# Second biases added while mixing by products over 128 rows, scales for eight tiles at once, output gates carried in the record

## The chip, the core and the metric

The kernel is one program on one core of a Trainium2 chip. A core has TensorE (PE; its weight loads are PEld), VectorE (DVE), ScalarE (ACT), GpSimd (POOL) and SyncE (SP, which here only issues DMAs). The metric is the device time of one execution in microseconds (us), lower is better.

## The reference

Eight sequences of 512 tokens with 256 features pass through one block: `x + s * g`. `s` is a recurrent attention layer with 16 heads of 16, `g` a mixture of eight experts, two per token.

```python
xn = _layernorm(x)
# attention: per token and head
q = silu(xn @ Wq); k = l2_norm(silu(xn @ Wk)); v = xn @ Wv
f = sigmoid(xn @ Wf1 @ Wf2);  a = -k * sigmoid(xn @ Wgamma) * f
def step(S):                    # 512 steps, one after the other
    S = S * f[..., None]
    S = S + k[..., None] * ((a @ S) + v)[..., None, :]
    return S, q @ S             # o
o = o * sigmoid(xn @ Wog1 @ Wog2)                 # the output gate
s = (o - mean(o)) * rsqrt(var(o) + 1e-5) * norm_w @ Wo
# experts: the two best of softmax(xn @ Wg + bg), weights cw
y = sum_e cw[:, e] * (gelu(xn @ W1[e] + b1[e]) @ W2[e] + b2[e])
g = silu((y - mean(y)) / sqrt(var(y) + 1e-5) * gamma + beta)
return x + s * g
```

## The kernel before

A **tile** is 128 tokens: 16 consecutive time steps of the eight sequences; there are 32. The recurrence has partition = (sequence, head), so its 512 steps are serial. DVE takes two steps at once: a **pair** g, 256 of them, eight to a **chunk** c of 16 time steps (`two_steps` L1167 to pair 55, `two_shared_steps` L1207 after it, where POOL computes the products of the state with decay, a and q, L310 to L327). Chunk c of the recurrence has the same tokens as tile c.

**Head.** Per tile, PE projects, ACT and DVE form a record of five rows of 16 (a, f, k, q, v), which SP writes to DRAM (`spill`, L362) and reads back in the recurrence's layout (`load_chunk`, L370). The output gate goes to DRAM by itself (`og_d`, L364). A record slot is used again four tiles later, so ACT and DVE wait for the write of tile n-4. From tile 4 on, this work stands between the operations of pairs 0 to 28. Then DVE routes the tokens (`route`, L1037), POOL scatters them to the experts' rows and the experts start.

**Experts.** 39 tiles of 256 rows: PE multiplies by W1 (L891), ACT applies gelu, PE multiplies by W2 (L903) and adds b2 as a product with one row of ones (L905); ACT scales the result by the token's weight (L723); POOL writes it to its token's row (`land`, L522). POOL runs its own list in order, so *when* it lands a result is a table in the code: landing number `landed` stands after the products of the first pair with (g-56)*PAIR_STEP >= landed//2*LAND_STEP, one per pair. A table of when, not a wait: POOL does it there, no earlier.

**Mixing and output**, woven into pairs 224 to 255. For each j of 16 (two tiles): PE adds the two experts' rows (`add_experts`, L914), ACT takes mean and squares (`moments`, L757), POOL the scale (`spreads`, L533), ACT normalizes (`normed`), PE transposes, ACT applies silu with gamma and beta (`silu_g`), PE transposes back, ACT copies g out (`turned_back`). For each tile n: SP fetches o and the gate, DVE multiplies them (`gate_o`, L1104) and takes statistics (`out_stats`), every four tiles their spread (`out_spread`), POOL the scales (`out_scales`), ACT normalizes, PE transposes and multiplies by Wo (`out_rows`, L949, products L959), DVE multiplies with g (`gated`, L1118), POOL adds x (`sum_up`), SP stores. In pair 224+n DVE does gate_o(n) and out_stats(n), and gated(n-5): **the recurrence waits in pair 229 for the output row of tile 0**, in pair 230 for tile 1, and so on. After pair 255 the last tile's output follows alone.

Of the kernel before, what the change touches and what calls it, by code (L numbers as in the profile page):

```python
# [19 lines left out]
REC = 5 * HD  # L20
A_, F_, K_, Q_, V_ = (HD * n for n in range(5))
# [23 lines left out]
YR = 3  # L45
SR = 4
RB = 3
SHARED = 7
LAND0, LAND_STEP = 390.0, 15.9
PAIR_STEP = 3.7  # L50


def build(nc, x, wq, wk, wv, wgamma, wf1, wf2, wog1, wog2, norm_w, wo,
          wg, bg, w1, b1, w2, b2, gamma, beta, out):
    ctx = ExitStack()
    with ctx:
# [6 lines left out]
        def sem(name):  # L63
# [6 lines left out]
        og_d = nc.dram_tensor("og_d", [NT, P, D], F32, kind="Internal").ap()  # L70
# [19 lines left out]
        b2_sb = sb("b2_sb", [1, E, D])  # L90
# [21 lines left out]
        ogs = work[:, o1 + 6 * D:o1 + 10 * D].rearrange("p (u n) -> p u n", u=RS)  # L112
        ksq = work[:, o1 + 10 * D:o1 + 11 * D]
# [54 lines left out]
        oTs = xTs  # L168
        sel = gw[:, 0, :, :].rearrange("p t e -> p (t e)")
        b2_flat = b2_sb[:, :, :].rearrange("a e n -> a (e n)")  # L170
        f_on = work[:, 0:FR * D].rearrange("p (u d) -> p u d", u=FR)
        fog, fx, f_sg = (work[:, (FR + n * SL) * D:(FR + (n + 1) * SL) * D].rearrange("p (u d) -> p u d", u=SL)
                         for n in range(3))
# [23 lines left out]
        s_og = sem("s_og")  # L197
# [11 lines left out]
        s_ogd = [sem(f"s_ogd{n}") for n in range(RS)]  # L209
# [10 lines left out]
        s_b1t = sem("s_b1t")  # L220
        s_b1 = sem("s_b1")
# [30 lines left out]
        s_o = sem("s_o")  # L252
        s_od = [sem(f"s_od{n}") for n in range(OB)]
        s_fl = [sem(f"s_fl{n}") for n in range(SL)]
        s_mul = sem("s_mul")
# [25 lines left out]
        N_W, N_C = 10, 9  # L281
# [16 lines left out]
        def shared(g):  # L298
            return g // NP >= SHARED

# [31 lines left out]
        def _(sp):  # L332
# [21 lines left out]
            sp.dma_start(b2_sb[:, :, :], b2.rearrange("(a e) n -> a e n", a=1)).then_inc(s_c, 16)  # L354
# [4 lines left out]
            sp.wait_ge(s_pool0, 4)  # L359
# [13 lines left out]
            def store_chunk(c):  # L373
                sp.dma_start(o_w[c], obh[:, c % OB, :, :]).then_inc(s_od[c % OB], 16)

            def next_chunk(c):
                sp.wait_ge(s_o, (c + 1) * RING)
                sp.wait_ge(s_recd[(c + RB) % RS], 16 * ((c + RB) // RS + 1))
                load_chunk(c + RB, c % RB)

            for n in range(NT):
# [6 lines left out]
                done, at = divmod(n - HEAD + 1, NP)  # L388
# [10 lines left out]
            for u in range(RS):  # L399
                sp.wait_ge(s_ogd[u], 16 * (NT // RS))  # L400

            def fetch(n):
# [19 lines left out]
            for s in range((NCH - WOVEN) * NP):  # L422
# [6 lines left out]
                if s % NP == 0:  # L429
                    c = WOVEN + s // NP - 1  # L430
                    sp.wait_ge(s_o, (c + 1) * RING)
# [3 lines left out]
            sp.wait_ge(s_o, NCH * RING)  # L435
# [10 lines left out]
        def _(pool):  # L446
# [6 lines left out]
                      channel_multiplier=ZR, allow_small_or_imprecise_dtypes=True).then_inc(s_pool0, 1)  # L453
            pool.memset(ident[:, :], 0.0).then_inc(s_id, 1)
# [78 lines left out]
            def spreads(j):  # L533
                lo, hi = 2 * j, 2 * j + 2
                pool.wait_ge(s_sq, hi)
                pool.tensor_scalar(ysq[:, lo:hi], ysq[:, lo:hi], 1.0 / D, EPS, ALU.mult, ALU.add).then_inc(s_yp, 1)
                pool.wait_ge(s_yp, 2 * j + 1)
                pool.tensor_tensor(yrs[:, lo:hi], ysq[:, lo:hi], neghalf[:, lo:hi], ALU.pow).then_inc(s_yp, 1)
                pool.wait_ge(s_yp, 2 * j + 2)
                pool.wait_ge(s_ynm, j + 1)  # L540
# [29 lines left out]
            def prepare_part(c, part):  # L570

# [7 lines left out]
                qa = rows[:, :, Q_:Q_ + 4 * HD].rearrange("p n (s w) -> p n s w", s=2)[:, :, :, 0:HD]  # L579
                fk = rows[:, :, F_:F_ + 2 * HD].rearrange("p n (s w) -> p n s w", s=2)  # L580
# [11 lines left out]
            landed = 0  # L592
            for g in range(SHARED * NP, T // 2):
# [726 lines left out]
```

## Time and profile before

| | us |
|---|---|
| median of 3 runs | 1239.25 (1235.51 to 1239.74) |
| the profiled execution: its time | 1238.9 |
| its span in the trace | 1237.2 |
| DVE busy in it | 1119.4 (90%), 3502 instructions |
| PE busy | 938.7 (76%) |
| POOL busy | 918.9 (74%) |
| ACT busy | 395.7 (32%) |
| DMA | 202.60 MB, 163 GB/s over the span |

The span is what the trace covers; 1.7 us of the execution lie outside it. The trace lists each instruction with its start and duration; neighbours on one engine overlap a little, so the distance between two starts says more than a duration. "[0.65 <-POOL prod_a L310]" means that the engine stood idle for 0.65 us before the instruction and what ended that. The chain of waits follows the work that ended last backwards.

### The profile page before, as it was taken

To read this page: it belongs to the slowest core of one execution; us is meant where nothing else is said; L and a number is where in the kernel's file an instruction comes from. 1 tells how busy PE (TensorE), PEld (TensorE's weight loads), DVE (VectorE), ACT (ScalarE), POOL (GpSimd) and SP (SyncE) were. 2 spreads that over 40 slices of the span, in tenths; PEclk is the share of its full clock that TensorE was granted. 3 is DMA by queue.
4 is the path that set the end of the run, shared out by engine and by line. 5 is a ranking of instruction groups with operands and counts; after the bars stand their busy time and mean duration, and the time that the engine had idled before them with its cause. 6 is when DMAs were issued, how large, how long until landed. Compare 5 with 4: busy or idle time off the path is not lost.

```text
span 1237.2 us, 17465 instructions
## 1 busy us (share of the span) xinstructions
PE 938.7 (76%) x3773; PEld 683.6 (55%) x3774; DVE 1119.4 (90%) x3502; ACT 395.7 (32%) x1047; POOL 918.9 (74%) x902
## 2 busy tenths in 40 slices
PE   5798898100029999999999999999999934667663
PEld 2343343000018888778888777888878723445441
DVE  3799999999999999999999999999999995988882
ACT  3444444200003333332232223333322203554552
POOL 3766666367844888888888888888888884877762
PEclk9888988655559999999999999999999976777787
DMA  5666656553335666655666556666666427355322
GB/s 165 194 209 177 213 180 188 140 191 107 111 94 150 191 196 195 195 170 183 191 195 193 174 177 195 196 187 181 183 192 191 120 67 210 93 157 149 99 81 69
DMA packets 247251, 202.60 MB, mean 164 GB/s; under 512 B 141425, under 2 KB 225233, under 8 KB 247185
## 3 DMA queue, kind: packets, MB, share of 16 engines
q1 hardware_dynamic: 170146, 82.81, 25.5%
q10 hardware_dynamic: 70224, 100.49, 24.8%
q0 software_dynamic: 6816, 18.69, 4.6%
q14 instruction: 55, 0.45, 0.1%
q8 instruction: 10, 0.16, 0.1%
HBM read 139.42 MB, written 62.54 MB: 163 GB/s over the span
## 4 chain that ended last, share of the span: by engine, by line
POOL 36%; DVE 27%; issue 16%; PE 7%; DMA 6%; SPq 3%; ACT 3%; POOLq 0%; DVEq 0%; ACTq 0%
POOL prod_q L327 13%; POOL prod_a L310 12%; POOL y_d L530 5%; DMA rec_d<-work 4%; DVE obh L1164 3%; PE psA L959 3%; DVE ubuf L1180 3%; DVE prod_a L1175 2%; PE psF L921 2%; SPq L335 2%; DVE prod_q L316 1%; DVE prod_a L1198 1%; DVE state L1204 1%; DVE outer L1190 1%; POOL cross L583 1%
## 5 line engine op out<-in xcount | busy, mean ns | idle before, releaser
L310 POOL TENSOR_TENSOR prod_a<-state,rbh 128x512 f32<-128x512 f32 x200 | 254.7, 1274 | 96.2 <-DVE state L1237 74.0
L903 PE MATMUL psF<-wts,work 128*128 128x256 f32 x1248 | 289.1, 385 | 3.2 <-ACT work L712 2.0
L891 PE MATMUL psA<-xgT,wts 128*128 128x256 f32 x1248 | 282.3, 384 | 0.9 <-ACT xgT L706 0.8
L891 PEld LDWEIGHTS psA<-xgT,wts 128*128 128x128 f32 x1248 | 235.4, 191 | 45.1 <-issue 13.8
L903 PEld LDWEIGHTS psF<-wts,work 128*128 128x128 f32 x1248 | 230.8, 190 | 50.0 <-issue 16.5
L327 POOL TENSOR_TENSOR prod_q<-state,rbh 128x512 f32<-128x512 f32 x175 | 223.2, 1276 | 0.0
L1164 DVE TENSOR_REDUCE obh<-prod_q 128x16 f32<-128x272 f32 x512 | 217.6, 426 | 0.0
L712 ACT ACTIVATE work<-psA,b_sb 128x256 f32<-128x256 f32 x312 | 130.8, 470 | 162.3 <-PE psA L891 159.5
L1224 DVE TENSOR_REDUCE ubuf<-prod_a 128x16 f32<-128x272 f32 x200 | 86.0, 430 | 37.5 <-POOL prod_a L310 37.1
L723 ACT ACTIVATE work<-psF,work 128x256 f32<-128x256 f32 x78 | 36.9, 473 | 256.9 <-PE psF L905 256.9
L879 PE MATMUL psT<-ident,work 128*128 128x128 f32 x156 | 24.2, 279 | 119.2 <-DMA work<-xs_d 119.1
L484 POOL TENSOR_TENSOR rinv<-ssm,neghalf 128x16 f32<-128x16 f32 x32 | 100.3, 3134 | 2.7
L502 POOL DMA_INDIRECT xs_d<-x_acc,idx x64 | 79.2, 1237 | 19.5 <-issue 18.9
L1237 DVE TENSOR_TENSOR state<-psB,outer 128x256 f32<-128x256 f32 x200 | 84.2, 421 | 5.8
L1216 DVE TENSOR_TENSOR prod_a<-state,psT 128x256 f32<-128x256 f32 x200 | 83.8, 419 | 5.8
L879 PEld LDWEIGHTS psT<-ident,work 128*128 128x128 f32 x156 | 19.2, 143 | 125.6 <-issue 117.9
L530 POOL DMA_INDIRECT y_d<-work,ids x78 | 78.9, 1011 | 12.3 <-issue 10.0
L1219 DVE TENSOR_REDUCE psB<-prod_a 128x16 f32<-128x272 f32 x200 | 86.5, 432 | 0.0
L1222 DVE TENSOR_TENSOR psB<-rbh,psB 128x256 f32<-128x256 f32 x200 | 83.6, 418 | 0.0
L1230 DVE TENSOR_TENSOR psB<-prod_a,psB 128x256 f32<-128x256 f32 x200 | 83.4, 417 | 0.0
L1232 DVE TENSOR_TENSOR outer<-rbh,psB 128x256 f32<-128x256 f32 x200 | 82.4, 412 | 0.0
L845 PE MATMUL psA<-w_kq,xTs 128*128 128x512 f32 x128 | 78.4, 743 | 0.0
(171 smaller groups left out, 1543.3 us busy)
## 6 DMA issues: line engine op xcount, KB each, us to landing
wts<-in_L_ffn_W_dram ACTq DMA_DIRECT2D x78, 1024.0 KB
rec_d<-work SPq DMA_DIRECT2D x32, 640.0 KB
rbh<-rec_d SPq DMA_DIRECT2D x32, 640.0 KB
xs_d<-zero SPq DMA_DIRECT2D x26, 387.0 KB, 9.0
work<-xs_d ACTq DMA_DIRECT2D x39, 258.0 KB
wts<-y_d ACTq DMA_DIRECT2D x16, 512.0 KB, 5.5
x_acc<-in_L_attn_x_dram SPq DMA_DIRECT2D x32, 128.0 KB
og_d<-work SPq DMA_DIRECT2D x32, 128.0 KB, 7.9
```

The source lines that it names most:

```text
L310: eng.tensor_tensor(prod_a[:, n, 1:3, :, 0:HD], state[:, g % SR, :, :].unsqueeze(1).broadcast_to(wide), rows.unsqueeze(2).broadcast_to(wid ...
L327: eng.tensor_tensor(prod_q[:, g % SR, :, :, 0:HD], state[:, g % SR, :, :].unsqueeze(1).broadcast_to(wide), rbh[:, u, 2 * n - 1:2 * n + 1, ...
L484: pool.tensor_tensor(rinv[:, u, :], ssm[:, u, :], neghalf[:, 0:H], ALU.pow).then_inc(s_ng, 1)
L530: pool.indirect_dma_start(y_d, bass.IndirectOffsetOnAxis(ids[:, v, q:q + 1], 0), ysb[v][:, q, :], None).then_inc(s_yd[v], 16)
L712: act.activation(hT[:, m, :], psA[m // 2 % 2][:, m % 2 * MT:(m % 2 + 1) * MT], ACT.Gelu, bias=b1_sb[:, bass.ds(e * FC + m, 1)]).then_inc(s ...
L891: mm = pe.matmul(psA[m // 2 % 2][:, m % 2 * MT:(m % 2 + 1) * MT], w1_sb[v][:, c, m * P:(m + 1) * P], xgT[:, c, :], start=(c == 0), stop=(c ...
L903: pe.matmul(psF[q][:, 0:D], hT[:, m, q * P:(q + 1) * P], w2_sb[v][:, m, :], start=(m == 0), stop=False)
L1164: dve.tensor_reduce(obh[:, c % OB, row % RING, :], prod_q[:, g % SR, side, :, :], AX.X, ALU.add).then_inc(s_o, 1)
L1216: dve.tensor_tensor(prod_a[:, n, 0, :, 0:HD], old, over_v(home_a[:, n, :]), ALU.mult).then_inc(s_chain, 1)
L1219: dve.tensor_reduce(u1, prod_a[:, n, 0, :, :], AX.X, ALU.add).then_inc(s_chain, 1)
L1224: dve.tensor_reduce(raw, prod_a[:, n, 2, :, :], AX.X, ALU.add).then_inc(s_chain, 1)
L1237: dve.tensor_tensor(new, home_o, outer[:, 1, :, :], ALU.add).then_inc(s_chain, 1)
```

## The change

1. **Second biases.** The one-row product per half expert tile (L905) and the register load for it go. Instead DVE forms the table of weights token x expert (two products and a sum in `route`), ACT spreads it, PE transposes it (during the scatter), and `add_experts` adds one more product per tile with all 128 rows: weights of four tiles' tokens against b2, which stands four times in `b2_sb` with zeros between. b2 is loaded by sixteen DMAs of eight rows in place of one, on SP's list, ahead of the first `spill`.
2. **Scales for eight tiles.** `spreads` takes eight tiles (four calls in place of sixteen), at pairs set by the table `SPREADS`. `moments` also copies the sums to `x_acc`, so `normed` reads them later. PE and ACT do the mixing in four quarters; **output rows begin in the last quarter**.
3. **Gates in the record.** The record has six rows. One product per chunk (`gate_outputs`) multiplies the chunk's outputs before they are stored: on DVE in chunks 1 to 7, on POOL after the products of each chunk's fourth pair from then on. `og_d`, its writes and reads, and `gate_o` go. A record slot is loaded again only after that product. POOL's `prepare_part` and `out_scales` move one pair later.
4. LAND_STEP 15.9 to 15.0 and PAIR_STEP 3.7 to 3.82: the last landing stands at pair 207 in place of 221.

```diff
-REC = 5 * HD
+REC = 6 * HD
+GQ = 8
+SPREADS = (612.0, 624.0, 640.0, 662.0)
+GATED = 3
-LAND0, LAND_STEP = 390.0, 15.9
-PAIR_STEP = 3.7
+LAND0, LAND_STEP = 390.0, 15.0
+PAIR_STEP = 3.82
+        def gate_outputs(eng, c):
+            eng.tensor_tensor(obh[:, c % OB, :, :], obh[:, c % OB, :, :], rbh[:, c % RB, :, O_:O_ + HD], ALU.mult)\
+                .then_inc(s_og, 1)
-            sp.dma_start(b2_sb[:, :, :], b2.rearrange("(a e) n -> a e n", a=1)).then_inc(s_c, 16)
+            sp.wait_ge(s_pool0, 5)
+            for n in range(P // E):
+                sp.dma_start(b2_sb[n * E:(n + 1) * E, n % 4, :], b2).then_inc(s_c, 16)
             def spill(n):
-                sp.wait_ge(s_og, n + 1)
-                sp.dma_start(og_d[n], ogs[:, u4, :]).then_inc(s_ogd[u4], 16)
             def store_chunk(c):
+                sp.wait_ge(s_og, c + 1)
             def fetch(n):
-                sp.dma_start(fog[:, n % SL, :], og_d[n]).then_inc(s_fl[n % SL], 16)
@@ POOL, after the products of pair g
-                if 3 <= g % NP < 6 and g // NP + 1 < NCH:
-                    prepare_part(g // NP + 1, g % NP - 3)
+                if g % NP == GATED and g // NP > SHARED:
+                    pool.wait_ge(s_o, g // NP * RING)
+                    gate_outputs(pool, g // NP - 1)
+                if 4 <= g % NP < 7 and g // NP + 1 < NCH:
+                    prepare_part(g // NP + 1, g % NP - 4)
                 s = g - WOVEN * NP
+                if spread < NT // GQ and ((g - SHARED * NP) * PAIR_STEP >= SPREADS[spread] or s >= 2):
+                    spreads(spread)
+                    spread += 1
-                        if s == hi - 1 and s < NT - 1:
+                        if s == hi:
                             out_scales(q)
-                    if s % 2 == 0:
-                        spreads(s // 2)
@@ ACT
-            moments(0)
-            for j in range(NT // 2):
-                normed(j)
-                ...
+            half = GQ // 2
+            for j in range(2 * half):
+                moments(j)
+            for q in range(NT // GQ):
+                act.wait_ge(s_yr, q + 1)
+                for j in range(q * half, (q + 1) * half):
+                    normed(j)
+                for j in range((q + 2) * half, min((q + 3) * half, NT // 2)):
+                    moments(j)
+                for j in range(q * half, (q + 1) * half):
+                    silu_g(j)
+                    ...
@@ PE
-                    pe.matmul(psF[q][:, 0:D], ones[0:1, :], b2_flat[:, bass.ds(e * D, D)], start=False, stop=True)\
-                        .then_inc(s_y, 1)
+                    mm.then_inc(s_y, 1)
             def add_experts(j):
+                    pe.matmul(total, cwT[:, n // 4, :], b2_sb[:, n % 4, :], start=True, stop=False)
+            for q in range(NT // GQ):
+                for j in range((q + 2) * half, min((q + 3) * half, NT // 2)):
+                    add_experts(j)
+                for j in range(q * half, (q + 1) * half):
+                    turn_y(j)
+                    turn_back(j)
+                    if q == NT // GQ - 1:
+                        for n in range(2 * (j % half), 2 * (j % half) + 2):
+                            out_rows(n)
+            for n in range(GQ, NT):
                 out_rows(n)
@@ DVE
-                if out_tile is not None and out_tile < NT - 1:
-                    gate_o(out_tile)
+                    if n == GATED and 0 < c <= SHARED:
+                        dve.wait_ge(s_o, c * RING)
+                        gate_outputs(dve, c - 1)
```

**What moves on PE.** Before, after the experts' last tile, one j in the middle of the mixing (L921 adds the experts, L933 and L943 are the transposes there and back, L953 and L959 the output row of one tile):

```order
L921 MATMUL psF<-wts,ident 128x256 x4
L933 MATMUL psT<-ident,wts 128x128 x4
L943 MATMUL psB<-ident,gT 128x128 x4
L953 MATMUL psT<-ident,work 128x128 x2
L959 MATMUL psA<-wo_sb,xTs 128x256 x2
L953 MATMUL psT<-ident,work 128x128 x2
L959 MATMUL psA<-wo_sb,xTs 128x256 x2
```

Now, the end of the third and the start of the fourth quarter on PE (L958 and L968 the transposes, L978 and L984 the output row):

```order
L958 MATMUL psT<-ident,wts 128x128 x4
L968 MATMUL psB<-ident,gT 128x128 x4
L958 MATMUL psT<-ident,wts 128x128 x4
L968 MATMUL psB<-ident,gT 128x128 x4
L978 MATMUL psT<-ident,work 128x128 x2
L984 MATMUL psA<-wo_sb,xTs 128x256 x2
L978 MATMUL psT<-ident,work 128x128 x2
L984 MATMUL psA<-wo_sb,xTs 128x256 x2
```

Two output rows followed every j, from the second on; now twelve j pass with none, four with two each, and 24 rows stand alone at the end. All additions of the experts stand ahead of the third quarter.

**What moves on POOL.** Pairs 226 and 227 before (L310 and L327 the products of a pair, L536 to L541 one `spreads` of two tiles, L583 the first `prepare_part`, L561 `out_scales`):

```order
L310 TENSOR_TENSOR prod_a<-state,rbh 128x32x16
L327 TENSOR_TENSOR prod_q<-state,rbh 128x32x16
L536 TENSOR_SCALAR ysq<-ysq 128x2
L538 TENSOR_TENSOR yrs<-ysq,neghalf 128x2
L541 TENSOR_TENSOR ysh<-ynm,yrs 128x2
L310 TENSOR_TENSOR prod_a<-state,rbh 128x32x16
L327 TENSOR_TENSOR prod_q<-state,rbh 128x32x16
L583 TENSOR_TENSOR cross<-rbh 128x8x2x16
L561 TENSOR_TENSOR rstd<-var,neghalf 128x4
L563 TENSOR_TENSOR shift<-nmean,rstd 128x4
```

An ordinary chunk on POOL now, from the fourth pair's products on (L318 and L335 are the products, L306 `gate_outputs`, L587 to L593 the parts of `prepare_part`):

```order
L318 TENSOR_TENSOR prod_a<-state,rbh 128x32x16
L335 TENSOR_TENSOR prod_q<-state,rbh 128x32x16
L306 TENSOR_TENSOR obh<-obh,rbh 128x256
L318 TENSOR_TENSOR prod_a<-state,rbh 128x32x16
L335 TENSOR_TENSOR prod_q<-state,rbh 128x32x16
L587 TENSOR_TENSOR cross<-rbh 128x8x2x16
L318 TENSOR_TENSOR prod_a<-state,rbh 128x32x16
L335 TENSOR_TENSOR prod_q<-state,rbh 128x32x16
L590 TENSOR_TENSOR rbh<-rbh 128x8x2x16
```

Three pairs of a chunk carried an extra product, now four in a row do. Of the four `spreads`, the last stands after the products of pair 226 and needs the squares of all 32 tiles.

## Rows read from the trace of the kernel before

**Rows 1.** The page, 40 slices of the span: DVE's busy tenths and TensorE's granted clock.
```profile
DVE  3799999999999999999999999999999995988882
PEclk9888988655559999999999999999999976777787
```

**Rows 2.** Timeline of DVE (start, duration): pairs alone, and first instructions of chunks 8 and 28.
```profile
721.54 0.42 DVE L1216 TENSOR_TENSOR prod_a<-state,psT 128x256 f32<-128x256 f32 x1
725.10 0.42 DVE L1216 TENSOR_TENSOR prod_a<-state,psT 128x256 f32<-128x256 f32 x1
...
414.46 0.38 DVE L1148 COPY prod_a<-rbh 128x256 f32<-128x256 f32 x1
...
1020.93 0.38 DVE L1148 COPY prod_a<-rbh 128x256 f32<-128x256 f32 x1
```

**Rows 3.** Timeline of one pair with a landing and a `prepare_part` on POOL.
```profile
701.60 1.01 POOL L530 DMA_INDIRECT y_d<-work,ids  x1 [0.17 <-issue]
...
702.64 0.73 POOL L583 TENSOR_TENSOR cross<-rbh 128x256 f32<-128x256 f32 x1
...
704.63 0.43 DVE L1224 TENSOR_REDUCE ubuf<-prod_a 128x16 f32<-128x272 f32 x1 [0.65 <-POOL prod_a L310]
```

**Rows 4.** Timeline of SP and DVE in the head.
```profile
28.62 0.45 SPq L354 DMA_DIRECT2D b_sb<-in_L_ffn_b_dram  x1
...
48.22 0.23 DVE L1130 TENSOR_TENSOR cross<-rbh 128x128 f32<-128x128 f32 x1
```

**Rows 5.** Chain of waits in the head (start, us, what).
```profile
31.45 6.50 DMA rec_d<-work
...
59.39 8.00 DMA rec_d<-work
```

**Rows 6.** Timeline of DVE in `route`.
```profile
246.57 0.42 DVE L1082 COPY tot<-psT 128x256 f32<-128x256 f32 x1 [1.16 <-PE psT L872]
```

**Rows 7.** Timeline of PE: an expert tile's start, a bias product and what follows, the mixing's start.
```profile
384.08 7.17 PE L891 MATMUL psA<-xgT,wts 128*128 128x256 f32 x32
...
719.04 0.69 PE L905 MATMUL psF<-b_sb,ones 1*128 x2
719.66 3.72 PE L903 MATMUL psF<-wts,work 128*128 128x256 f32 x16
...
1024.71 5.79 PE L921 MATMUL psF<-wts,ident 128*128 128x256 f32 x16 [23.94 <-DMA wts<-y_d]
```

**Rows 8.** Timeline of POOL: the last landing.
```profile
1012.60 1.01 POOL L530 DMA_INDIRECT y_d<-work,ids  x1 [0.17 <-issue]
```

**Rows 9.** Chain of waits in the mixing, one j.
```profile
1105.50 2.76 PE psF L921 x8
...
1110.41 0.92 ACT gT L784 x2
...
1111.37 1.11 PE psB L943 x4
...
1113.39 2.07 PE psA L959 x4
...
1116.36 1.76 PE psA L959 x4
```

**Rows 10.** Timeline of DVE among the output tiles, and pair 255's state.
```profile
1034.91 0.41 DVE L1237 TENSOR_TENSOR state<-psB,outer 128x256 f32<-128x256 f32 x1
...
1038.89 0.40 DVE L1237 TENSOR_TENSOR state<-psB,outer 128x256 f32<-128x256 f32 x1
...
1060.95 0.41 DVE L1123 TENSOR_TENSOR work<-psA,x_acc 128x256 f32<-128x256 f32 x1
...
1209.40 0.42 DVE L1237 TENSOR_TENSOR state<-psB,outer 128x256 f32<-128x256 f32 x1
```

**Rows 11.** Groups of instructions by line: busy us and mean ns of one.
```profile
L310 POOL TENSOR_TENSOR prod_a<-state,rbh 128x512 f32<-128x512 f32 x200 | 254.7, 1274 | 96.2 <-DVE state L1237 74.0 <-DVE psT L1141 21.0
L776 ACT ACTIVATE wts<-psF,ysh,yrs 128x256 f32<-128x256 f32 x32 | 16.4, 570 | 1.8 <-POOL ysh L541 1.7
```

More of the change, by code:

```diff
@@ L19 @@
 NTB = T // P
-REC = 5 * HD
-A_, F_, K_, Q_, V_ = (HD * n for n in range(5))
+REC = 6 * HD
+A_, F_, O_, K_, Q_, V_ = (HD * n for n in range(6))
 MT = 256
@@ L208, in build @@
         s_recd = [sem(f"s_recd{n}") for n in range(RS)]
-        s_ogd = [sem(f"s_ogd{n}") for n in range(RS)]
         s_gt = sem("s_gt")
@@ L591, in _ @@
             number(0)
-            landed = 0
+            landed = spread = 0
             for g in range(SHARED * NP, T // 2):
@@ L684, in _ @@
             act.wait_ge(s_b1, 1)
+            act.wait_ge(s_cw, 1)
+            act.activation(cw4.rearrange("p n (r k) -> p n r k", r=4),
+                           gw[:, 1, :, :].rearrange("p (n t) e -> p n (t e)", t=4).unsqueeze(2).broadcast_to([P, NT // 4, 4, 4 * E]),
+                           ACT.Copy).then_inc(s_cw4, 1)
+            act.wait_ge(s_cwT, 1)
+            for n in range(2):
+                act.activation(cwT[:, 4 * n:4 * n + 4, :].rearrange("p n t -> p (n t)"), psA[n][:, :], ACT.Copy, scale=0.25)\
+                    .then_inc(s_cws, 1)
             act.wait_ge(s_slot, 2)
@@ L688, in _ @@
                 act.wait_ge(s_recd[u], 16 * (NT // RS))
-            for u in range(RS):
-                act.wait_ge(s_ogd[u], 16 * (NT // RS))
             def expert_of(t):
@@ L760, in moments @@
                 for n in range(lo, hi):
-                    if j > 0:
-                        act.wait_ge(s_sq, n - 1)
-                    act.activation(junk[:, n % 2, :], summed(n), ACT.Copy, accum_out=ysum[:, n:n + 1]).then_inc(s_sum, 1)
+                    act.activation(x_acc[:, n, 0:D], summed(n), ACT.Copy, accum_out=ysum[:, n:n + 1]).then_inc(s_sum, 1)
+                if j % 2 == 1 and j // 2 + YR < NT // GM:
+                    load_y(j // 2 + YR)
                 act.wait_ge(s_sum, hi)
@@ L805, in _ @@
                 load_y(g)
-            moments(0)
-            for j in range(NT // 2):
-                normed(j)
-                if j % 2 == 1 and j // 2 + YR < NT // GM:
-                    act.wait_ge(s_yab, j + 1)
-                    load_y(j // 2 + YR)
-                if j + 1 < NT // 2:
-                    moments(j + 1)
-                silu_g(j)
-                if j > 0:
-                    for n in (2 * j - 2, 2 * j - 1):
+            half = GQ // 2
[9 more added lines that the diff above has]
+                    silu_g(j)
+                    if q < NT // GQ - 1:
+                        if j > q * half:
+                            turned_back(j - 1)
+                    else:
+                        n = 2 * (j % half)
                         out_normed(n)
+                        out_normed(n + 1)
                         out_turned(n)
-                turned_back(j)
-            for n in range(NT - 2, NT):
+                        turned_back(j)
+                        out_turned(n + 1)
+                if q < NT // GQ - 1:
+                    turned_back((q + 1) * half - 1)
+            for n in range(GQ, NT):
                 out_normed(n)
@@ L872, in _ @@
             pe.matmul(psT[1][:, 0:NT * E], ones[:, :], sel, start=True, stop=True).then_inc(s_cnt, 1)
+            pe.wait_ge(s_cw4, 1)
+            for n in range(NT // 4):
+                mm = pe.transpose(psA[n // 4][:, n % 4 * P:(n % 4 + 1) * P], cw4[:, n, :], ident[:, :])
+            mm.then_inc(s_cwT, 1)
             pe.wait_ge(s_slot, 2)
+            pe.wait_ge(s_cws, 2)
             def turn_rows(t, v, nth):
@@ L1284, in _ @@
             sum_row(T // 2, 0)
+            dve.wait_ge(s_o, NCH * RING)
+            gate_outputs(dve, NCH - 1)
             for n in range((NCH - WOVEN) * NP - LAG, NT - 1):
                 gated(n)
-            gate_o(NT - 1)
             out_stats(NT - 1)
```

105 lines of the change are left out of this document (48 added, 57 removed).

## The prediction

> **What bounds the kernel now.** First the page's slices [rows 1]: DVE is at nine tenths or more in 33 of 40, so the time is mostly the recurrence, one chain of 256 pairs on DVE. The slices that matter are the last seven, where DVE falls to eight tenths and TensorE's clock from 0.9 or more to 0.6 to 0.7. Then the timeline of DVE for the price of a pair. Alone it takes 725.10 - 721.54 = 3.56 us; from chunk 8 to chunk 28 it takes (1020.93 - 414.46) / 160 = 3.79 [rows 2], because a chunk adds its own small operations and because POOL is late when a landing and a `prepare_part` meet: 1.0 and 0.7 us beside the products, and DVE stands 0.65 us [rows 3]. In the last stage 26 pairs, from the first output row that DVE needs (`gated(0)`, pair 229, 1060.95) to pair 255's state (1209.40), take 148.5 us, 5.7 each, though a pair with its statistics and one more operation takes 1038.89 - 1034.91 = 3.98 [rows 10]. The chain of waits says why: there it runs through PE and ACT, the additions, the moments, silu, two transposes and two output rows one behind the other [rows 9]. After pair 255 come 1237.2 - 1209.8 = 27.4 us for the last tile.
>
> So the end is set by five terms: when pair 56 starts; when the last landing is made; from there to `gated(0)`; 26 pairs; 27.4 us.
>
> **Head: 9 us later.** b2 now takes sixteen DMAs on SP where it took one of 0.45 us [rows 4]; with the distance between such issues fifteen more are about 15 x 0.49 = 7.3 us, ahead of the first `spill`. The gate's own DMA goes (0.5). So record 0 leaves at 31.45 + 6.8 = 38.2 instead of 31.45, and takes 6.5 us [rows 5], perhaps 0.8 more for a sixth row. Its read-back starts at 45.5 instead of 38. Before, DVE began chunk 0 at 48.22 [rows 4], so the read-back took at most 10.2 us; if it takes 6, chunk 0 starts at 51.5. Behind it SP is serial for three tiles: record 3 left at 59.39 and landed 8.00 later [rows 5], and DVE's tile 7 (pair 3) waits for it. With 6.8 from the start, no gate DMA (0.5 a tile less) and a larger record it lands 6 to 7 us later. DVE has no idle time afterwards that would give this back [rows 1]. I take 6.5; bounds 1 (the read-back is quick and the queue drains faster without the gates) and 10. Six gate products on DVE ahead of pair 56, in chunks 1 to 6: 128x256 operations of 0.41 us [rows 10], a little less where they overlap their neighbours, 6 x 0.38 = 2.3. `route` gains four operations, three of 0.42 like the one in [rows 6] and smaller ones, some 1.6 us, but DVE stood 1.16 us for PE there: 0.4. Hidden elsewhere: the larger memset on POOL, ACT's joint sigmoid (one operation less), the transposes of the weight table, which lie beside the scatter. In all pair 56 starts 6.5 + 2.3 + 0.4 = 9 us later, bounds 3 and 13.
>
> The Trainium skill ("DMA: Bandwidth & Descriptors", Rules for kernel authors) says to coalesce small transfers, since below 64 KB mostly overhead is paid; here one transfer of 64 KB in total is split into sixteen of 8 KB. It speaks against this edit, and by its figure of some 2 us fixed for each, if they were serial, an estimate would be 30 us. The row bears out only an issue every half microsecond, and SP waits for none of them, so I keep 7.3.
>
> **Last landing: 37 us earlier.** A bias product costs PE 719.66 - 719.04 = 0.62 us [rows 7], two per tile, 1.25. The 38 tiles from 384.08 to the experts' end at 1024.71 - 23.94 = 1000.8 took 16.2 each; they will take 15.0. But POOL lands by its table: the last landing ended at 1012.60 + 1.01 = 1013.6 [rows 8], in pair 221, 13 us behind PE. It now stands in pair 207: 14 pairs or 53.1 us earlier. Against that 9 us from the head, and slower pairs: the gate product makes four of eight pairs heavy instead of three, 0.73 us [rows 3] on a POOL that has 3.56 - 2 x 1.27 = 1.0 us beside its two products [rows 11] and often a landing of 1.0 in it; half of it reaches DVE, 0.36 us a chunk, 0.045 a pair (bounds 0 and 0.09), 151 x 0.045 = 6.8. Last landing 1013.6 - 53.1 + 9 + 6.8 = 976.3. From there to the first addition took 1024.71 - 1013.6 = 11.1 [rows 7, 8]: 987.4, 37 us earlier than before.
>
> **From the first addition to `gated(0)`: 106 us instead of 36.** This is what the change pays. Before, output row 0 followed the second j. Now eight `moments` come first. PE needs 12 products per j in place of 8, 1.5 times the 2.76 of [rows 9], less when the clock is up, 2.7 to 4.1; with two cold ones 26.5 for eight. Eight `normed`: 0.57 each [rows 11], started 0.47 apart, 3.9. Four more `moments` 10.4. Four times silu and both transposes: per j 0.92 for silu, 0.7 to 1.1 for the way back [rows 9], as much for the way there, 0.6 for the copy of g, which PE waits for (an estimate, as for a `normed`): 3.4, and 13.6 plus a table load: 14. Second quarter 3.9 + 9.8 + 12.8, third 3.9 + 12.8, then 3.9 + 1.0 for the first silu and 3.6 for norm, transpose and product of row 0. Sum 106.6; bounds 97 (3.0 per silu cycle, warm) and 118 (3.9 and cold additions). `gated(0)` at 987.4 + 106.6 = 1094, where it was at 1061. DVE gets to pair 229 some 20 us before and stands. The last `spreads` holds POOL at pair 226 until the 32nd square, 30 us before that: it costs nothing, because pair 229 waits longer.
>
> TensorE's clock was 0.9 and more of full speed through the experts and 0.6 to 0.7 in this stage [rows 1]. The Trainium skill ("TensorE: Matmul & The Clock Gate", What's actually happening) has it that the throttled state is the default and activity lifts it. The trace agrees; with the long run of silu cycles, where PE idles more than before, its rule would lean to the upper bound of 118.
>
> **26 pairs: 115 us instead of 148.5.** `gate_o` is gone, with it its waits for the gate's transfer; per pair remain statistics and `gated`: 3.98 [rows 10], 103.5. Six or seven spreads of seven small operations, each under the 0.23 of [rows 4] and overlapping by half, 0.7 together: 4.5. Three chunks with 30.32 - 28.5 = 1.8 us each beyond the pairs [rows 2]: 5.4 (30.32 is eight pairs at 3.79, 28.5 eight at 3.56). For `out_scales` beside a gate or `prepare_part` on POOL 1.5. Sum 115. PE keeps up: without the additions two rows and a j cost about 8.5, 4.2 a row, and later 1116.36 - 1113.39 = 3.0 a row [rows 9]. Bounds 110 and 130. Pair 255's state at 1094 + 115 = 1209, before 1209.4.
>
> **The rest: 27.4 us.** `gate_outputs(31)` comes before the store and `gate_o(31)` goes after the fetch, both 0.4. Bounds 26 and 29.
>
> Sum: 987.4 + 106.6 + 115 + 27.4 = 1236.4 as span, 1238 with the 1.7 us outside it. The profiled execution had 1238.9 and the runs a median of 1239.25. Forecast 1238: 37 us won by the earlier landing are spent on rows that start 70 us later after it, and what the faster pairs give (33) goes on the same account.
>
> **Rivals.** *Faster: the mixing runs warm and the head hides its DMAs.* Then the head costs 3, the stage to `gated(0)` 97 and the pairs 111: 6 + 9.6 + 4 = 19.6 less, 1218; with half of this 1228. For it: single pieces of PE at twice the speed of others in [rows 9] (1.76 beside 2.07, 1.11), record 3's 8 us. Against: the clock digits.
>
> *Slower: the scales come too late for every group of four.* `out_scales` moved from pair hi-1 to hi, and `gated(lo)` stands at the end of hi+1. From the state before pair hi: products 2.5, a part 0.7, scales 1.4, normalize 0.65, transpose, copy and product 3.0, hand-overs 0.5: 8.8, against 0.7 + 2 x 3.98 = 8.7 for DVE. If POOL is one product late or PE cold, DVE waits 1.5 to 3 us in six or seven groups: +15, 1253. It decides from about 0.3 us of lateness on. For it: POOL's lateness in [rows 3]; against: the rows' product was as often 1.76.
>
> *Slower: the experts don't get faster*, because the rows' loads set the tile's length. Then the landings wait on POOL, the last is at about 1010, `gated(0)` 25 to 30 later: 1265. For it nothing in these rows: a bias product has the next product 0.62 behind it [rows 7], so PE goes straight on, and its clock stays up through the stage [rows 1].
>
> **How the numbers follow.** About 0.5% or 6 us is what a measurement of this kernel can tell from no change, so same is 1233 to 1245.5. Forecast 0.47, its own range 1228 to 1248 (0.35 same, 0.06 faster, 0.06 slower). Warm and hidden 0.28 (0.25 faster, 0.03 same). Late scales 0.14 (0.12 slower, 0.02 same). Experts no faster 0.06, slower. The other 0.05: 0.02, 0.01, 0.02. Faster 0.33, same 0.41, slower 0.26. The range reaches into both sides, 1221 to 1254.
>
> **What would show it.** Chunk 0 starting at 51 to 52 on DVE; pair 56 at 394; expert tiles 15.0 apart; last landing at 976; DVE idle 20 us or more in pair 229, ended by PE's output row near 1094; then 4.4 us a pair and no wait for a transfer of o. Wrong if `gated(0)` is at 1080 or earlier, if DVE waits in each group of four for PE, or if landings wait for ACT.

## The result, and the profile after

| | before | after |
|---|---|---|
| median us | 1239.5 (1235.5 to 1241.7, 4 runs) | 1257.6 (1255.6 to 1260.0, 4 runs) |
| profiled execution: time, span | 1238.9, 1237.2 | 1258.4, 1256.7 |
| ratio of the runs | | 1.015, 95% interval 1.013 to 1.017 |

The change makes the kernel 18 us slower. The forecast was 1238, the range 1221 to 1254: both missed, the range by 4 us.

The page after, the lines that answer [rows 1]:

```profile
DVE  3769999999999999999999999999999996479993
PEclk9778889655559999999999999999999687566656
```

Before, DVE was at five tenths in slice 34 and at eight in slices 36 to 39. Now the hole runs over slices 34 to 36 (six, four and seven tenths), and DVE is at nine tenths again from slice 37 on. (The prediction counted 33 slices at nine tenths in the kernel before; there are 32.) PE's clock falls one slice earlier, in slice 32, and is at five or six tenths from slice 35 on, where it was at seven or eight. The timelines (start, duration) give the five terms. First the head, SP and DVE, against [rows 4, 5]:

```profile
28.76 5.84 SPq L364 DMA_DIRECT2D b_sb<-in_L_ffn_b_dram  x16
36.55 0.63 SPq L375 DMA_DIRECT2D rec_d<-work  x1
44.08 0.38 SPq L378 DMA_DIRECT2D rbh<-rec_d  x1
46.34 0.60 SPq L375 DMA_DIRECT2D rec_d<-work  x1
54.98 0.38 SPq L378 DMA_DIRECT2D rbh<-rec_d  x1
...
49.28 0.29 DVE L1158 TENSOR_TENSOR cross<-rbh 128x128 f32<-128x128 f32 x1 [0.83 <-DMA rbh<-rec_d]
...
65.73 0.69 DVE L1041 TENSOR_TENSOR work<-psA,work 128x512 f32<-128x512 f32 x1 [3.25 <-DMA rec_d<-work]
...
78.29 0.69 DVE L1041 TENSOR_TENSOR work<-psA,work 128x512 f32<-128x512 f32 x1 [6.59 <-DMA rec_d<-work]
...
397.28 0.42 DVE L1242 TENSOR_TENSOR prod_a<-state,psT 128x256 f32<-128x256 f32 x1
```

Chunk 0 starts only 1 us later, but SP's list is serial for three tiles: write a record, wait for it to land, read it back. DVE then waits 3.25 and 6.59 us for records to land, pair 3 starts at 78.89 instead of 68.37, and pair 56 (last row) at 397.28 instead of 385.06: 12.2 us. Then the experts, the last landing and the first addition, against [rows 7, 8], and `gated(0)` and the last state, against [rows 10]:

```profile
391.11 7.07 PE L919 MATMUL psA<-xgT,wts 128*128 128x256 f32 x32
405.36 7.07 PE L919 MATMUL psA<-xgT,wts 128*128 128x256 f32 x32
...
980.88 1.01 POOL L535 DMA_INDIRECT y_d<-work,ids  x1 [0.17 <-issue]
...
988.91 1.22 PE L947 MATMUL psF<-b_sb,w_kq 128*128 128x256 f32 x2 [22.06 <-DMA wts<-y_d]
...
1104.85 0.42 DVE L1151 TENSOR_TENSOR work<-psA,x_acc 128x256 f32<-128x256 f32 x1 [23.09 <-PE psA L984]
...
1230.43 0.42 DVE L1263 TENSOR_TENSOR state<-psB,outer 128x256 f32<-128x256 f32 x1
```

| term | forecast | measured |
|---|---|---|
| head: pair 56 later by | 9 | 12.2 |
| a pair from chunk 8 to 28 | 3.84 | 3.84 |
| end of the last landing | 976.3 | 981.9 |
| from there to the first addition | 11.1 | 7.0 |
| first addition to `gated(0)` | 106.6 | 115.9 |
| `gated(0)` to pair 255's state | 115 | 125.6 |
| from there to the end of the span | 27.4 | 26.3 |

The last two rows count from the start of pair 255's state. The forecast's 27.4 was read from its end; measured in that way the last row is 25.9.

Where the additional 10.6 us of the 26 pairs are is seen at the end of a group of four tiles. DVE and POOL there:

```profile
1132.51 0.41 DVE L1151 TENSOR_TENSOR work<-psA,x_acc 128x256 f32<-128x256 f32 x1
1132.84 1.11 DVE L1009 TENSOR_TENSOR lt<-stats 128x4 f32<-128x4 f32 x1
1133.87 0.15 DVE L1010 TENSOR_TENSOR lt<-stats 128x4 f32<-128x4 f32 x1
1133.94 1.23 DVE L1011 TENSOR_TENSOR lt<-stats 128x4 f32<-128x4 f32 x1
1135.10 0.15 DVE L1013 SCALAR_TENSOR_TENSOR lt<-lt 128x4 f32<-128x4 f32 x1
1135.17 0.70 DVE L1016 TENSOR_SCALAR nmean<-lt 128x4 f32<-128x4 f32 x1
...
1136.05 0.41 DVE L1242 TENSOR_TENSOR prod_a<-state,psT 128x256 f32<-128x256 f32 x1
...
1132.67 1.26 POOL L318 TENSOR_TENSOR prod_a<-state,rbh 128x512 f32<-128x512 f32 x1
1133.88 1.27 POOL L335 TENSOR_TENSOR prod_q<-state,rbh 128x512 f32<-128x512 f32 x1
1135.12 0.73 POOL L587 TENSOR_TENSOR cross<-rbh 128x256 f32<-128x256 f32 x1
...
1139.85 1.27 POOL L318 TENSOR_TENSOR prod_a<-state,rbh 128x512 f32<-128x512 f32 x1 [1.59 <-DVE state L1263]
...
1140.01 0.41 DVE L1242 TENSOR_TENSOR prod_a<-state,psT 128x256 f32<-128x256 f32 x1
```

This spread of seven operations on four numbers per partition takes 1136.05 - 1132.84 = 3.2 us. Three of the seven are long, and each ends where an operation of POOL ends: 1133.95 beside 1133.93, 1135.17 beside 1135.15, 1135.87 beside 1135.85. The seven spreads between `gated(0)` and pair 255's state take 1.8, 3.2, 2.7, 3.2, 2.7, 2.7 and 2.7 us, 19.1 in all: where POOL has fewer operations beside a spread, or shorter ones, fewer of the seven are long. In the kernel before the same seven took 0.15 each, 0.7 in all:

```profile
1071.83 0.14 DVE L981 TENSOR_TENSOR lt<-stats 128x4 f32<-128x4 f32 x1
1071.90 0.15 DVE L982 TENSOR_TENSOR lt<-stats 128x4 f32<-128x4 f32 x1
...
1072.43 0.17 DVE L1116 TENSOR_SCALAR var<-lt 128x4 f32<-128x4 f32 x1
...
1072.68 1.01 POOL L561 TENSOR_TENSOR rstd<-var,neghalf 128x4 f32<-128x4 f32 x1 [3.61 <-DVE var L1116]
```

The last row tells why: before, POOL stood during the spread, because `out_scales` was next in its list and waits for it. The change moves `out_scales` a pair later, so POOL runs the next pair's products beside the spread.

The Trainium skill ("SBUF — State Buffer", Who interferes with whom) says that a DVE instruction with two inputs in SBUF contends with a GpSimd instruction that reads SBUF, that a `tensor_scalar` in a two-port mode can contend with GpSimd too, and that the one that comes second waits for the whole of the other. The trace agrees, at 1.11, 1.23 and 0.70 us: POOL's operation had begun each time, while L1010, which began just ahead of POOL's L335, took 0.15. The recurrence's operation that reads one of its inputs from PSUM keeps its 0.41 beside POOL's product (the last two rows).

### The profile page after: what moved, and what is told of

It reads as the page before. It is cut to its first block, busy times and chain, and to the rows that moved or that the text cites. A ratio compares the mean times of both kernels' runs of the same rounds, so it can differ in the third digit from the quotient of the medians.

```text
span 1256.7 us, 16942 instructions
## 1 busy us (share of the span) xinstructions
PE 911.4 (73%) x3689; PEld 688.8 (55%) x3689; DVE 1122.4 (89%) x3482; ACT 402.7 (32%) x1018; POOL 926.2 (74%) x891
## 4 chain that ended last, share of the span: by engine, by line
POOL 35%; DVE 33%; issue 17%; PE 4%; DMA 4%; ACT 3%; SPq 3%; POOLq 0%; DVEq 0%; ACTq 0%
POOL prod_q L335 13%; POOL prod_a L318 10%; POOL y_d L535 5%; DVE obh L1192 4%; DVE ubuf L1208 3%; DVE prod_a L1203 3%; DMA rec_d<-work 2%; SPq L343 2%; DVE prod_a L1226 1%; DVE state L1232 1%; DVE prod_q L324 1%; DVE work L1041 1%; DVE outer L1218 1%; PE psB L968 1%; DVE psB L1245 1%
## 5 line engine op out<-in xcount | busy, mean ns | idle before, releaser
L318 POOL TENSOR_TENSOR prod_a<-state,rbh 128x512 f32<-128x512 f32 x200 | 254.4, 1272 | 115.4 <-DVE state L1263 89.6
L930 PE MATMUL psF<-wts,work 128*128 128x256 f32 x1248 | 279.1, 383 | 0.0
L919 PEld LDWEIGHTS psA<-xgT,wts 128*128 128x128 f32 x1248 | 237.4, 192 | 44.8 <-ACT work L725 12.3
L930 PEld LDWEIGHTS psF<-wts,work 128*128 128x128 f32 x1248 | 236.9, 192 | 30.8
L335 POOL TENSOR_TENSOR prod_q<-state,rbh 128x512 f32<-128x512 f32 x175 | 222.0, 1269 | 0.0
L868 PE MATMUL psA<-w_kq,xTs 128*128 128x512 f32 x128 | 81.8, 773 | 0.0
```

What stands on the lines that cost most here:

```text
L318: eng.tensor_tensor(prod_a[:, n, 1:3, :, 0:HD], state[:, g % SR, :, :].unsqueeze(1).broadcast_to(wide), rows.unsqueeze(2).broadcast_to(wid ...
L335: eng.tensor_tensor(prod_q[:, g % SR, :, :, 0:HD], state[:, g % SR, :, :].unsqueeze(1).broadcast_to(wide), rbh[:, u, 2 * n - 1:2 * n + 1, ...
L919: mm = pe.matmul(psA[m // 2 % 2][:, m % 2 * MT:(m % 2 + 1) * MT], w1_sb[v][:, c, m * P:(m + 1) * P], xgT[:, c, :], start=(c == 0), stop=(c ...
L930: mm = pe.matmul(psF[q][:, 0:D], hT[:, m, q * P:(q + 1) * P], w2_sb[v][:, m, :], start=(m == 0), stop=(m == FC - 1))
```

## The experiments

Every edit is against the kernel after unless said. Times are medians; kernels that ran together share their runs of before (1240.0, 1240.6, 1240.0, 1242.0).

**1 and 2: b2's sixteen transfers.** Once taken out of the way, once put into the kernel before.

```diff
 late_b2
-            for n in range(P // E):            # ahead of spill(0)
-                sp.dma_start(b2_sb[n * E:(n + 1) * E, n % 4, :], b2)
+                if 8 <= n < 12:                # behind spill(n)
+                    for k in range(4 * (n - 8), 4 * (n - 8) + 4):
+                        sp.dma_start(b2_sb[k * E:(k + 1) * E, k % 4, :], b2)
 before_b2x16, in the kernel before
+            for n in range(P // E):            # ahead of spill(0)
+                sp.dma_start(wts[n * E:(n + 1) * E, n % 4 * D:(n % 4 + 1) * D], b2)
```

> The kernel after, with the sixteen b2 transfers moved on SP's list from ahead of the first record to behind records 8 to 11, four each. Theory (SP's queue): the issues hold record 0 back by 5.1 us and everything on the recurrence behind it; chunk 0 starts near 48.3, pair 3 near 73, pair 56 at 391 to 392 instead of 397.3, and the time falls by 5 to 6 us to 1252. Rival (the larger record): the sixth row makes each record's write slower and SP serial; then pair 56 moves by 0 to 2 us and the time is 1256 to 1258.

> The kernel before, with sixteen more transfers of b2 (into a part of the experts' weight buffer that is unused then) on SP's list ahead of the first record; nothing else. SP's queue alone: 16 x 0.37 = 5.9 us, less 0 to 1 of slack; pair 56 at 390 to 391 instead of 385.1 and the time 1244 to 1246. If DMAs are hidden: 1239 to 1241. If they were the whole of the head's 12.2 us: 1250.

Measured: 1252.2 (1.010 of before, 1.008 to 1.011), 5.4 less than after; and 1244.8 (1.0043, 1.0030 to 1.0056), 4.8 more than before. Pair 3 starts at:

| | b2 once or late | sixteen ahead |
|---|---|---|
| record of five rows | 68.37 | 75.11 |
| record of six rows | 72.22 | 78.89 |

Sixteen transfers cost 6.7 us with either record, the kernel with the sixth row 3.8 us with either list. Of the 6.7 us, 5.3 (kernel after) and 5.9 (kernel before) are record 0's later start on SP; the later records then took longer to land (46.36 to 54.02 instead of 40.34 to 47.51, for one), and why is open. Of the sixth row the timelines of SP show the price itself: records 0, 1 and 2 take 7.5, 8.1 and 8.0 us from issue to read-back in late_b2, and 6.5, 7.2 and 7.0 in the kernel before. Pair 56 follows: 391.81 in the kernel before with the transfers, 390.69 in the one after without. What is left to 385.06 is 5.6: 3.8 of the record, and 1.8 of the gate products and `route`. The effects on the time (4.8 and 5.4) are smaller than those on pair 56 (6.7 and 6.6). In before_b2x16 `gated(0)` is 6.2 us later and pair 255's state 4.2, so the last stage takes up 2 us; in late_b2 pair 255's state is 7.3 us earlier, and 1.2 of it go again behind that pair.

**3 to 6: the spread beside POOL.** The statistics by an aggregating operation that writes PSUM, on after and on before; the same seven operations at another place; and `out_scales` back where it was.

```diff
 psum_stats (before_agg: the same in the kernel before)
-                spread(lo, hi, s_fs, 6 * q)
-                dve.tensor_scalar(var[:, lo:hi], lt[:, 2, 0:hi - lo], 1.0 / D, EPS, ...)   # waits left out here and below
+                for n in range(lo, hi):
+                    dve.bn_aggr(oag[:, n - lo, :], stats[:, n, :])      # oag in psT[1]
+                dve.tensor_scalar(nmean[:, lo:hi], oag[:, 0:hi - lo, 0], -1.0, None, ALU.mult)
+                dve.tensor_scalar(var[:, lo:hi], oag[:, 0:hi - lo, 1], EPS, None, ALU.add)
 spread_moved: out_spread(q) from behind gated() to behind out_stats(), ahead of the pair's state
 scales_back
-                        if s == hi:
+                        if s == hi - 1 and s < NT - 1:
                             out_scales(q)
```

> The kernel after, with the spread of o's statistics (seven small operations on SBUF per four tiles) replaced by one aggregation per tile into PSUM and two small operations that read PSUM. Theory (SBUF operations of DVE wait for POOL's products): a spread falls from 3.2 us to about 0.8, seven times 2.3 us, and the time by 13 to 16 us to about 1243. Rival (late scales): the rows of each group are then not ready and DVE waits for PE at each group's first gated: at most 4 us gained, 1253 or more. Rival (the small operations are slow by themselves): no change, 1257.

> The kernel before, with o's statistics aggregated into PSUM as in the run on after. There a spread takes 0.8 us, because DVE waits for PE ahead of gated and POOL is done by then. Theory: no gain, 1238 to 1241. Rival (the aggregating form is worth 14 us anywhere): 1226.

> The kernel after, with the same seven small operations of each spread of o moved on DVE by one place, from behind gated (where POOL's two products of the next pair run) to ahead of the pair's state (where POOL has done its products and at most gates or sums). Theory (an operation of DVE with all its operands in SBUF waits until POOL's running one ends): most spreads take 0.7 to 1.5 instead of 3.2 us, the time falls by 10 to 15 us to 1243 to 1247. Rival (the gain of the aggregating version came from its fewer instructions): a spread takes 3 us as before, no change, 1257.

> The kernel after, with out_scales on POOL back in pair hi-1, as in the kernel before: POOL then waits for the spread instead of running the next pair's products beside it. Expected: the spread takes 0.7 us instead of 3.2, but POOL then does scales and a sum (2.0 us) ahead of the products, and DVE waits 1.4 us for them and some 0.6 in the next pair, as in the kernel before; of 2.5 us per group 0.5 is left, 2 to 5 us in all, 1252 to 1256. Rival (the shift by one pair is the whole cost): 1240 to 1244. Late scales by themselves (DVE waiting for PE) are not seen in either.

Measured: psum_stats 1243.9 (1.0033, 1.0021 to 1.0044), 13.7 less than after; from `gated(0)` to pair 255's state it takes 111.5 us, in after 125.6. The rival of late scales falls with it: with the spreads short, DVE waits 1.0 us for a row at the first group and hardly at the others. before_agg 1240.8 (1.0006, 0.9996 to 1.0017), nothing gained, as expected, though the reason given was not the right one: POOL was idle there because it waited for the spread. spread_moved 1248.4 (1.0072, 1.0058 to 1.0085), 9.2 less. scales_back 1253.3 (1.010, 1.008 to 1.012), 4.3 less. The timeline of DVE in psum_stats at such a place:

```profile
1130.19 0.41 DVE L1156 TENSOR_TENSOR work<-psA,x_acc 128x256 f32<-128x256 f32 x1
1130.52 0.37 DVE L1145 BATCH_NORM_AGGREGATE psT<-stats 128x2 f32<-128x6 f32 x4
1130.92 0.16 DVE L1147 TENSOR_SCALAR nmean<-psT 128x4 f32<-128x4 f32 x1
1131.00 0.15 DVE L1148 TENSOR_SCALAR var<-psT 128x4 f32<-128x4 f32 x1
1131.12 0.42 DVE L1247 TENSOR_TENSOR prod_a<-state,psT 128x256 f32<-128x256 f32 x1
```

0.6 us beside the same products of POOL. In spread_moved the seven old operations are short again where they stand among POOL's last operations of the pair; the first waits 0.28 until POOL's sum ends at 1130.17:

```profile
1129.44 0.73 POOL L573 TENSOR_TENSOR work<-work 128x256 f32<-128x256 f32 x1
1129.45 0.42 DVE L1138 BATCH_NORM_STATS2 stats<-work 128x6 f32<-128x256 f32 x1
1129.90 0.28 DVE L1009 TENSOR_TENSOR lt<-stats 128x4 f32<-128x4 f32 x1
1130.11 0.15 DVE L1010 TENSOR_TENSOR lt<-stats 128x4 f32<-128x4 f32 x1
```

So the seven operations are not slow by their number or by themselves; they are slow beside POOL's long ones. The run gained less than psum_stats, though its spreads are as short (0.7 to 0.8): from `gated(0)` to pair 255's state it takes 115.7 us. The spread now stands ahead of the state that POOL's next products wait for, and `out_scales` then comes ahead of a pair's products. In the group of these rows, from one state to the next, the pair with the spread takes 4.89 us and the second one after it 4.58 (with a wait of 0.52 for POOL), where 3.97 is usual; in psum_stats one pair of a group takes 4.58. scales_back has the spread at 0.7 us, and pays on the other side, for products that come late, as the kernel before did:

```profile
1131.31 0.17 DVE L1009 TENSOR_TENSOR lt<-stats 128x4 f32<-128x4 f32 x1
...
1132.18 1.02 POOL L566 TENSOR_TENSOR rstd<-var,neghalf 128x4 f32<-128x4 f32 x1 [1.81 <-DVE var L1144]
...
1135.49 0.44 DVE L1250 TENSOR_REDUCE ubuf<-prod_a 128x16 f32<-128x272 f32 x1 [1.70 <-POOL prod_a L318]
```

From one `gated` to the next there: 6.46 us at the group's end (1130.98 to 1137.44), in after 7.17 (1132.51 to 1139.68). In this group the shift of `out_scales` lost 0.7 us: the stall it made is 2.5, the stall it removed 1.8. From state to state the loss is 0.2 to 1.1 us in each of the seven groups, 4.6 in all, which fits the 4.3 of the time. So the long spreads cost 13.7 against a version without any stall, and only 4.3 against the old place of `out_scales`.

**7: TensorE's clock in the silu cycles.**

```diff
 fillers
             def turn_back(j):
+                if j < 12:
+                    for n in range(2):
+                        pe.matmul(psA[n % 2][:, 0:D], ident[:, :], b2_sb[:, n, :], start=True, stop=True)
                 pe.wait_ge(s_gT, KC * (j + 1))
```

> The kernel after, with two more products of 256 columns on PE in each of the first twelve j of the mixing (b2's table by the identity into psA, read by nobody), in the time in which PE waits for silu. Theory (TensorE's clock sizes the silu cycle): the granted clock stays at full speed there, a cycle takes 2.8 instead of 3.6 us, gated(0) comes 6 to 9 us earlier and the time falls to 1248 to 1252. Rival (ACT and the hand-overs size the cycle): no change in gated(0), or later by the products' own time; 1257 or more.

Measured: 1252.4 (1.010, 1.008 to 1.012), 5.2 less than after. Windows of after, then of this run (length; busy us and count of PE, PEld, DVE, ACT, POOL; granted clock, DMA share, GB/s):

```profile
1036.00:1052.00 16.00, 8.28 (x32) 6.89 (x33) 15.79 (x52) 8.33 (x17) 13.36 (x15) 0.57 0.09 28
```

```profile
1036.00:1052.00 16.00, 12.29 (x62) 10.28 (x63) 15.79 (x53) 10.56 (x21) 13.37 (x14) 0.89 0.09 28
```

The granted clock of the stretch rises from 0.57, near the lower level of 1.2 GHz, to 0.89, and a cycle (one transpose back to the next) falls from 3.63 us (1042.32 to 1045.95) to 2.76 (1041.48 to 1044.24). `gated(0)` is at 1096.83, 8.0 earlier; 2.5 us of it go again behind pair 255. Four transposes take 0.60 to 0.66 us at the upper level and 1.06 to 1.12 at the lower.

**8 to 12: the order of the mixing.** The old order with the new biases, gates and landings; then output rows from the second quarter on; then with the last spreads later; all that gained, together; and rows one pair later.

```diff
 rows_early (late_spreads, all_four, all_lag6 too)
+ROWS = (0, 0, 0, 0, 1, 1, 1, 1, 1, 1, 1, 1, 2, 2, 2, 2)       # output rows behind the j-th turn_back
-                    if q == NT // GQ - 1:
-                        for n in range(2 * (j % half), 2 * (j % half) + 2):
-                            out_rows(n)
+                    for n in range(sum(ROWS[:j]), sum(ROWS[:j + 1])):
+                        out_rows(n)
     ...                         # ACT's list in the same order
 late_spreads (all_four, all_lag6 too)
-SPREADS = (612.0, 624.0, 640.0, 662.0)       ... or s >= 2)
+SPREADS = (612.0, 624.0, 640.0, 700.0)       ... or s >= 6)
 old_mixing: moments, normed, spreads, turn_y and their loops as in the kernel before
 all_four: rows_early, late_spreads, psum_stats and late_b2
 all_lag6: all_four, and LAG = 5 becomes 6
```

> The kernel after, with the mixing's order of before (spreads for two tiles at a time on POOL at every second pair, additions one j ahead, two output rows behind each j) but with the bias product, the gates in the record and the landing table of after. Theory (PE and ACT per pair bound that order, 5.7 us a pair before, now 0.5 to 1 more for two cold bias products per j): DVE waits at rows all through, 1250 to 1260; the quarters are then no loss in themselves. Rival (the quarters are the loss): gated(0) near 1060 and no later waits, 1235 to 1240.

> The kernel after, with output rows from the second quarter of the mixing on: one per j in quarters two and three, two per j in the last, sixteen alone at the end. Theory (the order of the mixing sets gated(0)): row 0 is done near 1070, DVE comes to pair 229 near 1082 and does not stand 23 us there; the time falls by 18 to 23 us to 1235 to 1240. Rival (PE and ACT can't keep a row and a j in a pair's 4 us): the wait returns as waits at later rows, less than 8 us gained, 1250 or more.

> The run with the output rows from the second quarter on, and in addition the last spreads of the mixing on POOL behind the products of pair 230 instead of 226, where it held POOL and so DVE for 10.9 us. Theory: the wait goes and what is late next is row 0 at 1066 to 1072; 7 to 10 us less than that run, 1228 to 1231. Rival (PE's rows are the bound there): the wait returns at the rows, 1236 or more.

> All four edits together on the kernel after: rows from the second quarter on, the last spreads at pair 230, o's statistics aggregated into PSUM, b2's transfers behind records 8 to 11. If they add up: 1257.6 - 19.8 - 9 - 13.7 - 5.4 = 1210. If PE's rows become the bound of the last stage, only a part of the 13.7 is left: 1218 to 1224. Either is faster than both kernels.

> The kernel with all four edits, and in addition each row of o taken one pair later (gated(n) in pair 224+n+6). DVE waited 6.6 us for PE there at pairs 229 to 236; a pair later the rows should be ready. The one row more behind the recurrence is 1.8 us on a PE that stands 8.4 us before the last row. Theory: 5 to 6 us less, 1208 to 1210. Rival (the rows fall behind further, or the tail grows by its row): 1212 to 1216.

| run | us | ratio to before | `gated(0)` | pair 255's state |
|---|---|---|---|---|
| after | 1257.6 | 1.015 (1.013 to 1.017) | 1104.85 | 1230.43 |
| old_mixing | 1250.3 | 1.008 (1.006 to 1.010) | 1066.43 | 1221.05 |
| rows_early | 1237.8 | 0.998 (0.997 to 0.999) | 1078.91 | 1210.60 |
| late_spreads | 1230.5 | 0.992 (0.990 to 0.994) | 1068.61 | 1200.68 |
| all_four | 1214.2 | 0.980 (0.978 to 0.982) | 1060.62 | 1184.13 |
| all_lag6 | 1211.5 | 0.977 (0.976 to 0.979) | 1064.24 (pair 230) | 1181.83 |

old_mixing came out at its theory's time, but not by its mechanism. From 1040 to 1236 DVE waits little for rows and much for POOL, which waits for ACT's squares before each `spreads` of two tiles:

```profile
DVE ubuf L1238 <- POOL prod_a L318: 28.7, 10, 5.1
DVE work L1139 <- PE psA L975: 6.8, 4, 3.7
...
POOL ysq L541 <- ACT junk L780: 35.8, 12, 5.3
```

With spreads for eight tiles, early rows and the last spreads late (late_spreads) the time is 19.8 us below old_mixing. So the spreads for eight tiles go with a gain, and what the change lost is the late start of the rows that came with them; how much of the 19.8 is the spreads' own was not tested. rows_early removes the wait of 23 us and leaves this one, in pair 226:

```profile
1066.28 0.43 DVE L1246 TENSOR_REDUCE ubuf<-prod_a 128x16 f32<-128x272 f32 x1 [10.90 <-POOL prod_a L319]
```

It was in after too (12.8 us), where it cost nothing; here late_spreads wins 7.3 us by taking it away. all_four, at 1214.2, comes close to the 1210 at which the four gains add up. It keeps waits for rows (eight of 0.4 to 3.6 us up to 1116, 13.2 in all), and PE's granted clock falls beside them from 0.79 (1056 to 1072) to 0.55 (1104 to 1120); that the clock is their cause was not tested. all_lag6 is 2.7 us lower in the median, half of what its theory said, and the two intervals just overlap, so the gain is not sure. Its waits for rows there fall to four with 9.2 in all, but behind pair 255's state DVE waits 15.7 us for PE, in all_four 10.8.

## Why the prediction was wrong

- **"Head: 9 us later": the right mechanism, mis-sized.** The issues took 5.84 us, 0.37 apart and not 0.49, but with the serial list behind them the transfers cost 6.7 (6.5 was taken for them and the record together). The sixth row was given 0.8 for one write. It takes about 1.0 more in each, and three writes and read-backs stand one behind the other on SP ahead of record 3: 3.8. The gate products and `route` cost 1.8, and 2.7 was taken. 12.2 lies in the stated bounds of 3 to 13. (b2 is 8 KB, not the 64 KB in total that the prediction gives; the sixteen transfers carry 128 KB.)
- **"Last landing: 37 us earlier": right.** 35.8 by the first addition. A pair's price was right to 0.01 us. PE's tiles took 14.25 at first, less than the 15.0, and 15.2 on average, with waits for their rows (18.1 us in twelve waits); POOL's table set the landings, as said.
- **"From the first addition to `gated(0)`: 106 us": 9.3 short, within its bounds.** 5.2 is one term that was missing: the first eight tiles' squares are ready at 1014.8, but POOL takes `spreads(0)` only behind the products of pair 217, where the table has it (1017.68), and needs 2.2 us for it. In ACT's timeline:

```profile
1019.96 1.59 ACT L790 ACTIVATE wts<-x_acc,ysh,yrs 128x256 f32<-128x256 f32 x3 [5.19 <-POOL ysh L546]
```

  Most of the rest stands where PE is at the lower clock: the cycles were priced at 3.4 us and took 3.63, and the four additions in the first quarter took 12.3 with their moments instead of 10.4. The seventh experiment shows what the clock is worth there: `gated(0)` came 8 us earlier, 0.5 of it by an earlier first addition.

  The Trainium skill ("TensorE: Matmul & The Clock Gate", What's actually happening) was cited with the throttled state as the default, and as leaning to the upper bound of 118. The trace agrees: 115.9, at a granted clock of 0.57 in the silu cycles.
- **"DVE gets to pair 229 some 20 us before and stands", and the last spreads "costs nothing, because pair 229 waits longer": right**, 23.09 us in pair 229 and 12.8 in pair 226.
- **"26 pairs: 115 us": the step that failed is "Six or seven spreads of seven small operations ... 0.7 together: 4.5".** 0.7 is what a spread takes in the trace of before, but beside a POOL that stood. The change's own shift of `out_scales` puts POOL's products there, and the prediction did not ask what they would do to the spread. The seven spreads took 19.1 us, 14.6 more than the 4.5. Not all of it was additional: the chunks' own operations cost about 0.95 each, 2.9 and not 5.4, `out_scales` cost DVE nothing where 1.5 was priced, and a wait of 1.0 for PE came on top. 26 pairs at 3.97 (103.2), 19.1, 2.9 and 1.0 are 126.2, less about half a microsecond at the two ends: 125.6. That the transfer of the gate no longer holds DVE was right.
- **The rival "the scales come too late for every group of four" had the right shape for the wrong reason.** In after the row of a new group was ready 2 us ahead (its product ended at 1141.5, `gated` stood at 1143.64), and DVE waited once for 1.0 us. Each spread cost 2.1 us more than priced on average, within the 1.5 to 3 that the rival gives a group, but the loss was in the spread and not in a wait for PE. That its price and its 1253 come near is luck.
- **"Slower: the experts don't get faster" and "Faster: the mixing runs warm and the head hides its DMAs" were wrong.** The landings did not wait for ACT or PE; the head cost 12.2 us, and the clock was 0.57 in the silu cycles.

In sum: 3.2 of the head, 9.3 in the mixing, 10.6 in the pairs, less 4.1 between landing and addition and 1.1 at the end, with 2.4 of the landing later than the head explains: 20.3, and the span is 1256.7 instead of 1236.4. The head, the mixing and the pairs all erred to the same side, and the range was laid as if they were independent; without the 10.6 of the pairs, or without the 9.3 of the mixing, the time would have been in it. What stays open is why later records took longer to land behind the sixteen transfers.

## What to carry to other kernels

A duration read from a trace belongs to what ran beside it. When a change moves an operation of one engine, look at what it will now run beside on the others; here an operation of DVE with two inputs in SBUF, on four numbers per partition, took as long as POOL's on 512. A wait that costs nothing because a longer one follows is the first thing to look for once the longer one is gone: here 7.3 us. And where a change lets the first output appear only at the end of a long preparation, start the outputs within it: that was 20 us here. With the later last spreads, the statistics by way of PSUM and b2's transfers out of the way, the slower kernel became one 2% faster, with the same biases and gates.

## What the hardware showed

- Seven operations of 0.15 us on DVE took 2.7 to 3.2 us beside POOL's products of 1.27 us (1.8 in the shortest case), and 0.7 beside an idle POOL. Versions that read or write PSUM took 0.6 beside the same products.
- A direct transfer of 8 KB on SP had the next one behind it after 0.37 us. Sixteen of them ahead of the records made pair 3 start 6.7 us later.
- A record's write of 768 KB took about 7.5 us from issue to the read-back behind it (36.55 to 44.08), one of 640 KB 6.5 (31.45 to 37.97).
- More work for PE made the kernel 5 us faster: its granted clock was 0.89 instead of 0.57 from 1036 to 1052.
